# AdaLN with a modulated convolution and four feed-forward networks: the main convolution of layers 1 and 2 as three products for two outputs

## The reference

```
for i, typ in enumerate(('same', 'upsample', 'same', 'downsample')):   # the cond chain
    s = style @ mod_w[i].T + mod_b[i]
    w = SCALE * weights[i] * s;  w = w * rsqrt(sum(w * w) + EPS)        # per batch element
    out = conv (K = 3) of out with w, + bias; blur after 'upsample', before 'downsample'
x = x + FFN0(cond0(x))     # fp8-quantised dense 1024 x 1024
x = x + FFN1(cond1(x))     # dense + top-2 of 16 experts, rank 64
x = x + FFN2(cond2(x))     # dense + sparsemax over 8 experts, rank 16
x = x + FFN3(cond3(x))     # gated, rank 256, inner width 2752
```

## Time and profile before

| | |
|---|---|
| time, median of 3 runs | 2126.35 us (2123.62 to 2126.62) |
| span of the profiled execution | 2130.7 us |
| PE busy | 1993.7 us, 94% |
| DVE busy | 1154.0 us, 54% |
| ACT busy | 917.1 us, 43% |
| POOL busy | 373.8 us, 18% |
| mean granted TensorE clock | 0.973 |

### The profile page before, as it was taken

The page is one execution under the profiler, slowest core; times in us unless marked ns, Lnnn a source line. Parts: engine busy times, 40 slices in busy tenths (PEclk is TensorE's granted clock), DMA queues, the critical chain, the costliest instruction groups (busy, mean ns, idle before and its releaser), DMA issues. The chain is left out here.

```text
span 2130.7 us, 30321 instructions
## 1 busy us (share of the span) xinstructions
PE 1993.7 (94%) x9760; PEld 1664.5 (78%) x9768; DVE 1154.0 (54%) x1990; ACT 917.1 (43%) x1395; POOL 373.8 (18%) x457
## 2 busy tenths in 40 slices
PE   5799968799999979998999999998999999999999
PEld 4677734799999977887788888877888778878886
DVE  6888888655545544336544444446555433343333
ACT  4477754444444431003433333324666544433442
POOL 4122211111111100002111111112111222222221
PEclk9899989899999989999999999998999999999999
DMA  7566547322111243444211111113333211142114
GB/s 196 175 183 186 169 159 239 118 74 67 59 59 59 79 150 122 139 135 149 93 59 59 59 60 59 61 63 119 108 98 108 80 49 49 44 145 86 50 44 162
DMA packets 118606, 222.27 MB, mean 104 GB/s; under 512 B 18336, under 2 KB 65184, under 8 KB 117792
## 3 DMA queue, kind: packets, MB, share of 16 engines
q1 hardware_dynamic: 102048, 212.36, 31.3%
q10 hardware_dynamic: 16512, 9.31, 1.6%
HBM read 159.04 MB, written 62.59 MB: 104 GB/s over the span
## 5 line engine op out<-in xcount | busy, mean ns | idle before, releaser
L1040 PE MATMUL ps<-l_u_hi,l_g_hi 128*128 128x512 f32 x512 | 210.4, 411 | 20.8 <-DVE l_u_lo L1402 10.3
L1222 ACT ACTIVATE rows<-ps,l_EY,dem3e 128x512 f32<-128x512 f32 x128 | 99.2, 779 | 280.6 <-PE ps L1040 262.5
L1040 PE MATMUL ps<-l_u_lo,l_g_hi 128*128 128x512 f32 x512 | 205.5, 401 | 0.0
L1040 PE MATMUL ps<-l_u_hi,l_g_lo 128*128 128x512 f32 x512 | 205.3, 401 | 0.0
L123 POOL TENSOR_TENSOR rows<-l_EY,ones 128x4 f32<-128x4 f32 x128 | 37.4, 292 | 803.2 <-ACT rows L1222 803.2
L2413 DVE SCALAR_TENSOR_TENSOR f_prod<-ps,b,f_gate 128x512 f32<-128x512 f32 (+1 forms) x88 | 66.1, 751 | 172.3 <-ACT f_gate L2353 172.3
L2454 POOL TENSOR_TENSOR x_lo<-f_prod,x_hi 128x512 fp32r<-128x512 f32 (+1 forms) x88 | 105.0, 1193 | 292.2 <-ACT x_hi L2360 292.2
L2283 PE MATMUL ps<-pt_hi,v_hi 128*128 128x512 f32 (+1 forms) x352 | 138.5, 393 | 1.8 <-PEq L625 1.8
L1402 DVE SCALAR_TENSOR_TENSOR l_u_lo<-ps,s_u,l_u_hi 128x512 fp32r<-128x512 f32 x128 | 95.1, 748 | 83.1 <-ACT l_u_hi L1204 82.2
L2283 PE MATMUL ps<-pt_lo,v_hi 128*128 128x512 f32 (+1 forms) x352 | 138.5, 394 | 0.0
L1204 ACT ACTIVATE l_u_hi<-ps,s_u 128x512 fp32r<-128x512 f32 x128 | 87.8, 689 | 116.7 <-PE ps L983 70.6
(11 more groups left out here) (355 smaller groups left out, 5032.9 us busy)
## 6 DMA issues: line engine op xcount, KB each, us to landing
x<-rows SPq DMA_DIRECT2D x64, 512.0 KB, 2.9
xin<-x SPq DMA_DIRECT2D x96, 256.0 KB, 3.9
rows<-x SPq DMA_DIRECT2D x48, 512.0 KB, 4.3
out<-rows SPq DMA_DIRECT2D x32, 512.0 KB, 2.6
v<-in_ffn_v SPq DMA_DIRECT2D x84, 128.0 KB, 2.6
xin<-in_x SPq DMA_DIRECT2D x16, 512.0 KB, 5.5
xb<-in_x SPq DMA_DIRECT2D x16, 512.0 KB, 3.3
x<-xb SPq DMA_DIRECT2D x16, 512.0 KB, 2.6
```

Source lines behind the costliest of these rows:

```text
L1040: mm = nc.tensor.matmul(ps[:, 3 + h, :], Gs[ws][:, h, at:at + P], Us[ms][:, h, 1 + q:1 + q + HALF], start=(k == 0), stop=(k == 11))
L1222: nc.scalar.activation(hs[:, h, :], ps[:, 3 + h, :], ACT.Identity, bias=EY[:, 1, 0, bass.ds(h * NP + p, 1)], scale=dem3e[:, bass.ds(h * NP ...
```

## The change

In layers 1 and 2 (`FAST`), for pairs 1 to 15, the four-tap product is computed by the identity that gets two outputs of a two-tap filter from three products. With even and odd columns apart (256 each), PE computes for each h one shared product of the sums of weights with the even columns (6 matmuls of 256 columns, bank 2) and two products with differences of neighbouring columns (2 x 6 matmuls of 256 columns, bank 3 + h). The result is shared + product for the odd and for the even outputs. ACT and DVE have to form the sums of weights (`Cs`, `sums`), the even columns (`middle`, `Es`) and the differences (`gaps`, `HFs`), with their hi and lo parts; the scale `s_u` moves from u to the weights; DVE's `join_h` takes the place of ACT's `read_h`. What had been at the head of iteration p+1 (`read_a`, `split_x`, `split_z`) and the splits of u is now one block `lead(p+1)` that ACT and DVE run in iteration p ahead of `tail(p)`. In layer 2 the small chain (`gates`) is taken out of `tail` and put ahead of `lead`. Pair 0 keeps the old form. One staging slot is shared between tiles, a second batch of weight chunks goes ahead of `split_h(0)`, the load of the next layer's pack in layer 1 goes from the head to the last pair, and PE waits in the last pair of layer 1 for ACT's copy out of bank 2.

```diff
+FAST = (1, 2)
+QUART = HALF // 2
...
+            def main_fast_half(p, h, ahead):
+                pe.wait_ge(gl_ready, g0 + p + 1)
+                pe.wait_ge(ul_ready, 2 * (g0 + p) + 2)
+                if h == 0:
+                    pe.wait_ge(hl_ready, g0 + p)
+                    if ahead:
+                        pe.wait_ge(al_ready, 2 * (g0 + p) + 4)
+                    elif layer == 1:
+                        pe.wait_ge(sem("amax_all"), 2)
+                else:
+                    pe.wait_ge(md_ready, 2 * (f0 + p) + 1)
+                k = 0
+                for g in range(2):
+                    for ws, ms in PASSES:
+                        mm = nc.tensor.matmul(ps[:, 2, h * QUART:(h + 1) * QUART],
+                                              Cs[ws][:, h, (1 - g) * P:(2 - g) * P], Es[ms][:, h, g:g + QUART],
+                                              start=(k == 0), stop=(k == 5), skip_group_check=True)
+                        k += 1
+                mm.then_inc(md_done, 1)
+                for odd in range(2):
+                    k = 0
+                    for g in range(2):
+                        at = (6 - 2 * odd - 4 * g) * C
+                        for ws, ms in PASSES:
+                            mm = nc.tensor.matmul(ps[:, 3 + h, odd * QUART:(odd + 1) * QUART],
+                                                  Gs[ws][:, h, at:at + P],
+                                                  HFs[ms][:, h, odd, g:g + QUART],
+                                                  start=(k == 0), stop=(k == 5), skip_group_check=True)
+                            k += 1
                 mm.then_inc(m_done, 1)
...
@@ ScalarE @@
+            def read_u_fast(p):
+                act.wait_ge(c0_done, 2 * (g0 + p) + 2)
+                act.wait_ge(m_done, 2 * (g0 + p))
+                nc.scalar.activation(HFs[0][:, :, 0, QUART:QUART + 1], ps[:, 0:2, HALF - 1:HALF], ACT.Copy)
+                nc.scalar.activation(middle[:, :, :], ps[:, 0:2, 0:HALF:2], ACT.Copy).then_inc(uh_ready, 1)
+                act.wait_ge(uh_ready, 2 * (g0 + p) + 1)
+                nc.scalar.activation(Es[0][:, :, 0:QUART], middle[:, :, :], ACT.Copy)
+            def split_gaps(p):
+                act.wait_ge(sums_ready, 2 * (f0 + p) + 2)
+                nc.scalar.activation(HFs[0][:, :, :, 0:QUART], gaps, ACT.Copy).then_inc(uh_ready, 1)
+            def read_middle(p, h):
+                act.wait_ge(md_done, 2 * (f0 + p) + h + 1)
+                nc.scalar.activation(middle[:, h, :], ps[:, 2, h * QUART:(h + 1) * QUART], ACT.Identity,
+                                     bias=EY[:, 1, 0, bass.ds(h * NP + p, 1)],
+                                     scale=dem3e[:, bass.ds(h * NP + p, 1)]).then_inc(md_ready, 1)
+            def split_gc(p):
+                act.wait_ge(sums_ready, 2 * (f0 + p) + 1)
+                for h in range(2):
+                    nc.scalar.activation(Gs[0][:, h, :], g_f[:, h, :], ACT.Copy, scale=column(s_u, p, h))
+                    last = nc.scalar.activation(Cs[0][:, h, :], sums[:, h, :], ACT.Copy, scale=column(s_u, p, h))
+                last.then_inc(gh_ready, 1)
...
             def iteration(p, first, ahead):
-                if ahead:
-                    read_a(p + 1)
-                    split_x(p + 1)
-                if ahead > 1:
-                    split_z(p + 2)
-                read_h(p, 0)
+                (read_middle if fast else read_h)(p, 0)
                 if ahead:
                     cross_g(p + 1)
-                read_h(p, 1)
+                (read_middle if fast else read_h)(p, 1)
                 split_h(p)
+                if ahead and fast:
+                    split_gc(p + 1)
+                    lead(p + 1, ahead - 1)
...
@@ VectorE @@
+            def differ_u(p):
+                dve.wait_ge(uh_ready, 2 * (g0 + p) + 1)
+                dve.wait_ge(ul_ready, 2 * (g0 + p))
+                odd = ps[:, 0:2, 1:HALF:2]
+                v.tensor_scalar(gaps[:, :, 0, 0:1], middle[:, :, 0:1], -1.0, None, ALU.mult)
+                v.tensor_tensor(gaps[:, :, 0, 1:QUART], odd[:, :, 0:QUART - 1], middle[:, :, 1:QUART], ALU.subtract)
+                v.tensor_tensor(gaps[:, :, 1, :], odd, middle[:, :, :], ALU.subtract).then_inc(sums_ready, 1)
+            def read_u_fast(p):
+                dve.wait_ge(uh_ready, 2 * (g0 + p) + 2)
+                v.tensor_tensor(Es[1][:, :, 0:QUART], middle[:, :, :], Es[0][:, :, 0:QUART].bitcast(F32),
+                                ALU.subtract)
+                v.tensor_tensor(HFs[1][:, :, 0, QUART:QUART + 1], ps[:, 0:2, HALF - 1:HALF],
+                                HFs[0][:, :, 0, QUART:QUART + 1].bitcast(F32), ALU.subtract).then_inc(ul_ready, 1)
+                v.tensor_tensor(HFs[1][:, :, :, 0:QUART], gaps, HFs[0][:, :, :, 0:QUART].bitcast(F32),
+                                ALU.subtract).then_inc(ul_ready, 1)
+            def join_h(p, h):
+                dve.wait_ge(m_done, 2 * (g0 + p) + h + 1)
+                dve.wait_ge(md_ready, 2 * (f0 + p) + h + 1)
+                v.scalar_tensor_tensor(hs[:, h, :].rearrange("p (j r) -> p r j", r=2),
+                                       ps[:, 3 + h, :].rearrange("p (r j) -> p r j", r=2),
+                                       dem3e[:, bass.ds(h * NP + p, 1)],
+                                       middle[:, h, :].unsqueeze(1).broadcast_to([P, 2, QUART]),
+                                       ALU.mult, ALU.add).then_inc(hs_ready, 1)
+            def sum_c(p):
+                dve.wait_ge(g_summed, g0 + p + 1)
+                dve.wait_ge(gl_ready, g0 + p)
+                halves = g_f[:, :, :].rearrange("p h (g i m) -> p h g i m", g=2, i=2)
+                for h in range(2):
+                    last = v.tensor_tensor(sums[:, h, :].rearrange("p (g m) -> p g m", g=2),
+                                           halves[:, h, :, 0, :], halves[:, h, :, 1, :], ALU.add)
+                last.then_inc(sums_ready, 1)
+            def split_c(p):
+                for h in range(2):
+                    last = v.scalar_tensor_tensor(Cs[1][:, h, :], sums[:, h, :], column(s_u, p, h),
+                                                  Cs[0][:, h, :].bitcast(F32), ALU.mult, ALU.subtract)
+                last.then_inc(gl_ready, 1)
...
+            def lead(p, ahead):
+                if fast:
+                    differ_u(p)
+                if ahead:
+                    read_a(p + 1)
+                    if not fast:
+                        split_x(p + 1)
+                if ahead > 1:
+                    split_z(p + 2)
+                if fast:
+                    read_u_fast(p)
+                    if ahead:
+                        split_x(p + 1)
...
             def iteration(p, first, ahead):
...
+                if fast:
+                    join_h(p, 0)
...
+                    join_h(p, 1)
                 if ahead:
                     sum_g(p + 1)
+                    if fast:
+                        sum_c(p + 1)
...
                 split_h(p)
...
+                if ahead and fast:
+                    split_g(p + 1)
+                    split_c(p + 1)
+                    if layer == 2:
+                        gates(p)
+                    lead(p + 1, ahead - 1)
                 if layer > 0:
                     tail(p)
...
 @@ first_pair of ScalarE and of VectorE @@
-                some_chunks(1)
+                some_chunks(2 if fast else 1)
                 split_h(0)
```

More of the change, by code:

```diff
@@ L624, in conv_phase @@
     with_ffn = layer in (1, 2)
+    fast = layer in FAST
+    f0 = (NP - 1) * sum(l < layer for l in FAST) - 1
     with ExitStack() as ctx:
@@ L737, in staged @@
             src, dst, width = chunks[k]
-            flat = stage[:, k % SLOTS, 0:width]
+            slot = k % SLOTS
+            if layer == 2 and fast and slot == own_slot or layer == 3 and fast and slot == 1:
+                flat = shared[:, 0:width]
+            else:
+                flat = stage[:, slot - (layer == 2 and fast and slot > own_slot), 0:width]
             if len(dst[0].shape) == 3:
@@ L871, in iteration @@
                                  d["ffn0_w_halves"][bass.ds(p * P, P), :]).then_inc(half_loaded, 16)
+                if fast and layer == 1 and not ahead:
+                    sp.wait_ge(ul_ready, 2 * (g0 + NP))
+                    load_pack()
                 if with_ffn and not first:
```

212 lines of the change are left out of this document (155 added, 57 removed).

## The result

The changed kernel takes 2114.8 us, median of 10 runs (2108.2 to 2124.3), against 2125.6 us for the kernel before in 10 runs beside them (2123.6 to 2129.8): a ratio of 0.9945 with a 95% interval of 0.9931 to 0.9959. It is faster, by some 11 us or 0.5%; 19.2 us were forecast (2107 us). The profiled execution took 2111.6 us, of which 2109.6 are its span.

What follows compares the result with a forecast made beforehand. PE, at work for 94% of the span, was taken as the bound. -41.2 + 15 + 0.7 + 6.3 = -19.2 us gave 2107 us; the forecast's own range was 2095 to 2117, 8 in 10 2088 to 2130.

Steps and rivals of the forecast that it cites:

- PE's share: Halves of main, layers 1 and 2: 2.11 us in place of 2.80, 60 times, -41.2 us (-38 at the other end).
- Rival 4: Matmuls of 256 columns held up by 18 weight loads in place of 12; nothing saved, 2132 us; chance 0.03.
- The DVE chain of layer 1: PE waits about 1.1 us at `weights_g` for DVE's FFN sum in 13 pairs: +15 us (0 to +31).
- the start of POOL's addition: POOL's bias addition taken to start 7.9 us after the FFN's sum, holding `split_g` back by 0.9 us in layer 1.
- The DVE prices by element count: New strided and broadcast DVE operations, in no profile row, priced by element count, with half as much again as bounds.
- Layer 2's last six matmuls: PE waits about 0.05 us for `gsp` lo in 13 pairs of layer 2: +0.7 us (0 to +18).
- Once in a layer: Weight chunks in pair 0, 3.3 us wait in layer 2's first pair, 0.8 in layer 1's last: +6.3 us.
- the 0.8 for bank 2: Last pair of layer 1: PE waits 0.8 us for ACT's copy from bank 2.
- the 1.1 twice: Pair 0 of each layer: second weight chunk on DVE ahead of `split_h(0)`, for which PE waits, +1.1 us twice.
- Rival 3: POOL's addition falls amid DVE's SBUF-to-SBUF splits, costing 2.34 us a pair: slower, +26, 2152 us; chance 0.12.
- Rival 1: PE stays the bound everywhere, both DVE chains fit: 2089 us; chance 0.24.
- one split a pair stretched by POOL: Expected in the profile: POOL's bias addition lengthens one of DVE's splits in each pair.

Runs made afterwards that it cites:

- the version of 2091.8 us: On the version with POOL waiting, layer 2's first pair reordered and DVE's x splits moved, SP loads the residual before x: 2091.8 us, ratio 0.9844 to before.
- POOL waiting: Changed kernel, but POOL's bias addition also waits for DVE's sum of the next pair's third kernel matrix in layers 1 and 2: 2109.7 us, ratio 0.9908.
- the kernel with the meeting at the splits: Against the version with POOL waiting for the sum, POOL's bias addition waits for ACT's upper halves of the next pair's G and C: 2171.1 us.
- the second profile: Profile of the changed kernel run once more, unchanged: 2114.9 us, ratio 0.9936 to the kernel before.

## Why the prediction was right, and where it was not

The sign held, and 2114.8 us lies in the forecast's own range. The sum looks closer than it was: the two layers fell by 19.0 us in the first profile, and of the -19.2 forecast the 2.2 us for the weight chunks fall outside them, so that -21.4 is its like. Two terms were wrong by some 9 us each with opposite signs, and that they nearly cancel is luck.

- **PE's share** (-41.2 forecast) held. With every wait out of the way, pairs are 1.43 and 1.25 us shorter (24.32 to 22.89, 26.61 to 25.36), 0.67 us a half and -40 us for 60 halves. Of this the reorder gave 0.12 us a pair of layer 1; the columns alone are 0.64 us a half, -38 us, the forecast's other end, since a matmul of 256 columns costs 0.119 us, as the row of layer 3 had said, and not 0.1175. Rival 4 is out.
- **The DVE chain of layer 1** (+15) had the right mechanism and the wrong size. PE does wait at the second group for the FFN's sum, and the pair is longer by 23.36 - 22.89 = 0.47 us for it in the place of 1.1, +6 us. (The forecast's own figures, T + 20.2 less T + 19.2, make 1.0 us and +13.) The term that was mis-sized is the start of POOL's addition, taken as 7.9 us after the sum: it was 7.2 (611.25 to 618.49), so that the addition ended as the splits of G began. Of the 0.9 us by which it was to hold them back 0.11 are left (pairs of 23.36 us, 23.25 without the addition). The DVE prices by element count held: from the splits' start to the end of the sum the chain took 13.6 us (597.68 to 611.25), where 13.7 stood, and in the version of 2091.8 us `differ_u` takes 1.26 us from start to next start, where 1.28 stood. DVE's busy time was put too high all the same, 19 us a pair against 17.0.
- **Layer 2's last six matmuls** (+0.7): nothing in the middle pairs, right.
- **Once in a layer** (+6.3): the first pair of layer 2 is 4.5 us longer (28.5 to 33.1) though its columns give 1.3 back; PE waited there 1.23 us for hg and 2.93 for the gated factor, where 3.3 was forecast. That of layer 1 is 2.2 shorter, 0.7 more than its columns, and layer 1's last pair gives back 0.7 in place of 1.4 (22.3 to 21.6 without meetings), as the 0.8 for bank 2 said (0.73 us from the matmul whose result ACT copies to main's first). Together some +5 us inside the layers; the 1.1 twice lie outside them, as told above.
- **What was missed**: the same 0.7 us that took POOL's addition away from `split_g` brought it next to `sum_c`, which the change had put on DVE 0.8 us in front of it. In layer 2 the prediction's own figures left 0.7 us between the two (`sum_c` ends at T + 2.8, the addition starts at T + 5.9 less 2.4); they came at T + 3.3 and T + 2.7 (T = 1088.1 in the pair shown). The prediction had priced `sum_c` as work (0.66 us) and not asked what else it is: one more SBUF-to-SBUF operation in reach of POOL. Four meetings, two of them beside a wait that was there already: 1.85 + 1.85 in the middle of layer 2, 1.8 + 1.55 and 1.1 + 1.6 at the ends of the layers, +9.7 us. With these, -40 + 6 + 5 + 9.7 = -19.
- **Rival 3** named the right pair of engines and the right reason, and was under-priced: with the meeting at its own place the two layers take 36 us more than in the kernel before (799.9 against 763.9), where it had +26. The addition there costs 64.5 us against POOL waiting; the rival's like figure is 13 x (2.4 + 2.1) = 58. Its waits were sized well, and the clock behind eight of them added 8 x 1.5 = 12 us that it had not counted. **Rival 1** is what the last version shows to be possible: 2091.8 us, where it said 2089. It needs POOL held, the first pair reordered, the splits of x moved and the two loads on SP swapped; it was not what the change did by itself.

The forecast "one split a pair stretched by POOL" came out in layer 1 only in half of the pairs and by 0.1 to 0.4 us, and "wrong if PE waits at some other place" came true in four pairs.

## What to carry over

When an engine gets new work, list for each new operation not only its length but which memory it reads, and lay the other engine's long SBUF operation beside it: here 0.2 us more or less of a DMA's landing (an addition 0.18 or 0.37 us behind the sum's start) decided over 1.8 to 3.4 us, and a semaphore wait on the engine with slack made it certain. Give such an addition a place, rather than leave it to a DMA. When a step is moved, follow the DMA that it releases and what stands behind that on its queue; swapping two loads on SP was worth 10.9 us in the two layers (736.2 to 725.3). And compare stretches between two events of the same engine, not spans, where the rest of the program varies by 10 us; but look at what of the change lies outside them.

## What was not expected of the hardware

- The length of one late operand's wait doesn't settle whether the granted clock falls behind it. In the kernel with the meeting at the splits PE waited 2.27 us at the same line in two pairs of layer 1. Behind the wait that ends at 584.07 the windows shown above have the lower level, 1.2 GHz; behind this one the clock stays at the upper level (PE busy, granted clock):

```profile
637.84 0.53 PE L1059 MATMUL ps<-l_a_hi,c_hi 128*128 128x320 f32 x2 [2.27 <-DVE rows L1754]
```
```profile
638.00:640.00 2.00, 2.00 (x17) 1.00 0.65 258
```

  Of the twelve waits at this line eight, of 2.24 to 2.36 us, were followed by some 3 us at the lower level and four, of 2.25 to 2.35 us, were not. In the changed kernel 1.80 us left the clock up, and 2.04 us, ahead of the FFN at 1376.75, did not, as these windows of its first profile show; in the second profile 1.97 us at the same pair cost nothing behind it (23.30 in place of 24.87 us for the pair after).

```profile
1378.00:1380.00 2.00, 2.00 (x10) 0.50 0.00 0
1380.00:1382.00 2.00, 2.00 (x8) 0.67 0.03 8
```

  The price of such a wait is thus its length or its length and some 1.5 us more, and these rows don't tell which in advance.
- The two sums of `sum_c` show which of two engines goes first: at 1090.67 DVE had started 0.18 us before POOL; its first sum ended and its second stood until POOL's end at 1093.36. At 1118.37 the second sum ran already, and it was the addition that took 0.2 us longer. The Trainium skill, SBUF — State Buffer, section "SBUF: two separate sides", says that the first to start holds the shared ports for its whole instruction; the trace agrees. Operations of DVE that read PSUM were not touched (1.21 to 1.23 us beside POOL and alone).
